# Row sums of adj in the first layer: the running adds on GpSimd instead of VectorE

## What is computed

```python
def _L0_gnn_ref(h, adj, W_neigh, b_neigh, W_self, b_self):
    deg = jnp.sum(adj, axis=1, keepdims=True) + 1e-05
    h_neigh = (adj / deg) @ h
    return relu(h_neigh @ W_neigh.T + b_neigh + h @ W_self.T + b_self)

def _L1_gnn_ref(x, adj, W, b):
    rowsum = adj.sum(axis=1)
    d_inv_sqrt = jnp.where(rowsum > 0, rowsum ** (-0.5), 0.0)
    support = (d_inv_sqrt[:, None] * adj * d_inv_sqrt[None, :]) @ x
    return relu(support @ W + b)

x = _layernorm(x + _L0_gnn_ref(x, adj, ...))
x = _layernorm(x + _L1_gnn_ref(x, adj, ...))
```

## Time and profile before

| | us |
|---|---|
| median of 3 runs | 800.73 |
| lowest, highest | 800.4, 802.11 |
| span of the profiled execution | 800.8 |

### The profile page before, as it was taken

One profiled execution on the slowest core, in us unless ns is written; L12 is line 12 of the kernel. 1 busy time (PEld: TensorE's weight loads), 2 busy tenths in 40 slices (PEclk: granted clock), 3 DMA queues, 4 the chain that ended last, 5 costly groups with the idle time before them and its releaser, 6 DMA issues.

```text
span 800.8 us, 11034 instructions
## 1 busy us (share of the span) xinstructions
PE 782.1 (98%) x3704; PEld 653.0 (82%) x3704; DVE 577.4 (72%) x868; ACT 386.9 (48%) x528; POOL 0.3 (0%) x6
## 2 busy tenths in 40 slices
PE   7899999999999999999999999999999999999995
PEld 4678888888888888888888888888888888888884
DVE  5799989899898998989966554555546455554643
ACT  3463745536446364454554545445444544545451
POOL 0000000000000000000000000000000000000000
PEclk9999999999999999999999999999999999999998
DMA  8767574755647556465565575746575574657540
GB/s 258 274 252 239 179 244 154 253 183 166 236 155 236 193 174 236 157 233 189 181 227 165 175 255 174 250 162 237 180 236 187 171 246 162 236 180 239 180 158 27
DMA packets 54459, 160.93 MB, mean 201 GB/s; under 512 B 5024, under 2 KB 18464, under 8 KB 54432
## 3 DMA queue, kind: packets, MB, share of 16 engines
q1 hardware_dynamic: 46224, 152.46, 56.6%
q10 hardware_dynamic: 8208, 8.13, 2.9%
HBM read 152.17 MB, written 8.39 MB: 201 GB/s over the span
## 4 chain that ended last, share of the span: by engine, by line
PE 94%; DMA 2%; DVE 2%; ACT 1%; issue 0%; SPq 0%
PE ps_main L675 84%; PE ps_epi L613 8%; DMA raw<-adj_t 2%; PE ps_main L657 1%; PE ps_epi L634 1%; DMA tt<-x_nat 1%; DVE lo L389 0%; DVE acc L565 0%; ACT hi L256 0%; PE ps_epi L693 0%; DVE tt L436 0%; DVE stats L585 0%; DVE tt L419 0%; DVE xs L389 0%; ACT tt L359 0%
## 5 line engine op out<-in xcount | busy, mean ns | idle before, releaser
L256 ACT ACTIVATE hi<-raw 128x1024 fp32r<-128x1024 f32 x254 | 269.4, 1061 | 352.8 <-PE ps_main L675 327.8
L389 DVE TENSOR_TENSOR lo<-raw,hi 128x1024 fp32r<-128x1024 f32 x254 | 310.4, 1222 | 145.3 <-ACT hi L256 145.2
L675 PE MATMUL ps_main<-hi,xs 128*128 128x512 f32 x1136 | 366.3, 392 | 4.3 <-DVE lo L389 4.3
L675 PE MATMUL ps_main<-hi,zs 128*128 128x512 f32 x896 | 283.0, 390 | 0.0
L675 PEld LDWEIGHTS ps_main<-hi,xs 128*128 128x128 f32 x1136 | 214.2, 189 | 49.3 <-DVE lo L389 3.6
L675 PE MATMUL ps_main<-lo,xs 128*128 128x512 f32 x568 | 222.4, 392 | 0.0
L675 PEld LDWEIGHTS ps_main<-hi,zs 128*128 128x128 f32 x896 | 168.3, 188 | 34.3
L675 PE MATMUL ps_main<-lo,zs 128*128 128x512 f32 x448 | 174.7, 390 | 0.0
L565 DVE TENSOR_TENSOR acc<-acc,raw 128x1024 f32<-128x1024 f32 x112 | 136.3, 1217 | 0.0
L675 PEld LDWEIGHTS ps_main<-lo,xs 128*128 128x128 f32 x568 | 107.3, 189 | 20.0 <-issue 0.2
L675 PEld LDWEIGHTS ps_main<-lo,zs 128*128 128x128 f32 x448 | 84.2, 188 | 16.3
(11 more groups left out here) (74 smaller groups left out, 322.7 us busy)
## 6 DMA issues: line engine op xcount, KB each, us to landing
raw<-adj_t SPq DMA_DIRECT2D x256, 512.0 KB, 3.3
res<-x_nat SPq DMA_DIRECT2D x11, 512.0 KB, 6.4
xt_sb<-xt SPq DMA_DIRECT2D x8, 512.0 KB, 5.0
x_scratch<-tt ACTq DMA_DIRECT2D x8, 512.0 KB, 6.2
res<-x_scratch SPq DMA_DIRECT2D x8, 512.0 KB, 6.0
out<-tt ACTq DMA_DIRECT2D x7, 512.0 KB, 6.4
tt<-x_nat SPq DMA_DIRECT2D x4, 512.0 KB, 6.4
acc<-x_nat SPq DMA_DIRECT2D x2, 256.0 KB, 3.6
```

The costliest lines, as they stand in the source:

```text
L256: return act.activation(dst, src, ACT.Copy)
L389: return dve.tensor_tensor(dst, src, hi_part.bitcast(f32), ALU.subtract)
L675: last = pe.matmul(ps[:, f, :], stationary(layer, part, jt, f), mov[:, slot(u), cols], start=(jt == 0 and i == 0), stop=(jt == JT - 1 and ...
```

## The change

The 15 adds of each block in the first layer leave VectorE's program and stand in GpSimd's, in a loop of their own with the same arithmetic and order. Each now waits for its transfer (`raw_full`) and for the add before it. At the start of a block after the first, GpSimd waits for `rs_copied`, so that the half of acc which it takes has been read; for this rs_copied begins one higher (a memset that counts it), and TensorE's wait for it moves up by one. The first block's x goes through acc's second half on its way in, so GpSimd also waits for `xl_ready` and `unit_done` there. SP's and ScalarE's programs are the same as before.

```diff
-        marks = sb("marks", [P, 3])
+        marks = sb("marks", [P, 4])
...
             pool.memset(marks[:, 0:1], 0.0).then_inc(tt_stored, 16)
+            pool.memset(marks[:, 3:4], 0.0).then_inc(rs_copied, 1)
+
+            def one_block(layer, b, parity, epi):
+                if layer == 1:
+                    return
+                g0 = b * NU
+                k0 = b * (NU // RING)
+                a = acc[:, parity, :]
+                if not is_first(b):
+                    pool.wait_ge(rs_copied, b)
+                    pool.wait_ge(xl_ready, 1)
+                    pool.wait_ge(unit_done, WHOLE)
+                for u in range(NU):
+                    pool.wait_ge(raw_full[slot(u)], (k0 + (u // RING + 1)) * 16)
+                    if u == 1:
+                        pool.tensor_tensor(a, raw[:, slot(0), :], raw[:, slot(1), :], ALU.add)\
+                            .then_inc(acc_done, 2)
+                    if u > 1:
+                        pool.wait_ge(acc_done, g0 + u)
+                        pool.tensor_tensor(a, a, raw[:, slot(u), :], ALU.add).then_inc(acc_done, 1)
+
+            one_block(0, 0, 0, None)
+            with pool.Fori(1, NB - 1, 2) as b:
+                one_block(0, b, 1, None)
+                one_block(0, b + 1, 0, None)
+            one_block(0, NB - 1, 1, None)
...
                     place(u, 1)
-                    if layer == 0:
-                        a = acc[:, parity, :]
-                        if u == 1:
-
-
-                            dve.tensor_tensor(a, raw[:, slot(0), :], raw[:, slot(1), :], ALU.add)\
-                               .then_inc(acc_done, 2)
-                        if u > 1:
-                            dve.wait_ge(acc_done, g0 + u)
-                            dve.tensor_tensor(a, a, raw[:, slot(u), :], ALU.add).then_inc(acc_done, 1)
                     place(u, 2)
...
-                        pe.wait_ge(rs_copied, e + 1)
+                        pe.wait_ge(rs_copied, e + 2)
```

## The result

| | before | after |
|---|---|---|
| median, us | 800.65 | 883.51 |
| lowest, highest, us | 800.4, 802.11 | 880.73, 884.01 |
| span of the profiled execution, us | 800.8 | 882.2 |

The changed kernel is slower: the ratio is 1.1022, 95% interval 1.1005 to 1.1039. Some 83 us were lost. The forecast was 886 us, in a range of 845 to 905 us for this case alone and of 799 to 905 us overall.

A forecast was written before the change was run, and what follows sets the result against it. TensorE was taken as the bound. Alternating SBUF access adds 11.4 us in each of 8 blocks: 800.8 + 91 - 6 of used-up lead = 886 us; range 845 to 905 for this case, 799 to 905 overall.

The forecast's parts named there:

- VectorE's adds are worth nothing in seven blocks, 1.2 us in the first: First layer: removing VectorE's 120 adds saves 0 beside a full TensorE in seven blocks, 1.2 us in the first block.
- Turns: First layer: GpSimd adds and VectorE's two-SBUF-operand instructions alternate, so their times add up; 11.4 us more a block, chance 0.58.
- GpSimd's add, 2.22 us: Each moved add on GpSimd: two passes of 1.06 us plus 0.10 us, between ends of 1.22 and 3.18 us.
- Handing over, 2.4 us a block: First-layer block: some 30 passes between GpSimd and VectorE at 0.08 us each, 2.4 us in all.
- the sum of a block: First-layer block: VectorE's two-operand work 26.1, GpSimd's adds 33.3 and passes between engines 2.4, 61.8 us against 50.4.
- The first block, 11 us: First block of the first layer: its work ends at 71 us instead of about 60, the same 11 us loss.
- The lead of 6 us used up at the end: End of the first layer: the splits' 6.5 us of advance over TensorE is consumed instead of kept, -6 us.
- The span as the metric: Whole kernel: nothing is shown outside the profiled span, which equals the median to 0.1 us, so it stands for the metric.
- The signs: Profile after: adds 3 us and more on meeting, TensorE busy 50 of 62 us, lo waits 80 to 90, second layer 46.5.
- rival (c): First layer: the engines share SBUF in part, overlap 8 to 11 us, blocks 52 to 54, time 807 to 823; chance 0.10.
- six small instructions: VectorE in each first-layer block: newton, d_cur, d_all, nmr, inv_root counted as two-operand SBUF work, 0.16 us each, 1.0 in all.
- Rival (b): First block: the 3.13 us TensorE wait and lower clock go too, 795 us; chance 0.10, including no loss with a little more.

## Why the prediction was right, point by point

- **VectorE's adds are worth nothing in seven blocks, 1.2 us in the first.** Right: with GpSimd only writing, every block behind the first is 50.39 us as before, and 1.7 us are gained in all (799.2 us).
- **Turns.** Right, and shown in three ways: by the instructions' own lengths, by the width, and by reading against writing. The Trainium skill's rule (page "SBUF — State Buffer", section "Who interferes with whom": the one that starts first keeps the shared ports for its whole length) agrees with these rows, 3.47 us for a lo behind an add of 2.40. The instructions with one operand in PSUM, which I had left out of the sum, were never longer: 25 of the 32 of L455 began while an add was running, and none took over 0.418 us.
- **GpSimd's add, 2.22 us.** It is 2.40. This term was too small by 0.18 us, 2.7 us a block. Two passes came near: GpSimd's own copy of one operand takes 1.04 us, and twice that is 2.08. Whether the add really makes two passes is not shown. The estimate of 2.25 us from the Trainium skill (page "GPSIMD Engine Reference", section "Elementwise — side-by-side cycle accounting") is low as well; the measured 2.40 decides.
- **Handing over, 2.4 us a block.** Nothing of it shows. L462, 0.42 us alone, ends 0.28 us behind the add that it waited for, and VectorE's own instructions follow one another 1.14 us apart rather than 1.22. That makes the sum of a block 24.7 + 36.0 = 60.7 us where I had 61.8. The add was 2.7 us a block too short; the hand-overs, 2.4, and the distance of VectorE's instructions, 1.4, were too long. That these nearly cancel is luck. Six of the seven blocks measured 60.0 to 61.6 us.
- **The first block, 11 us.** 11.9 us between the spans, about 13 by the medians.
- **The lead of 6 us used up at the end.** The last of the seven blocks takes 56.6 us, the six ahead of it 60.9 on average, so 4.3 us were given back. That they are the lead is not shown.
- **The span as the metric.** The profiled execution of the changed kernel has a span of 882.2 us and a time of 884.01: 1.8 us lie outside it, which I had put at nothing. That the span before equalled the median was chance: its execution was about 2 us slower than the median.
- **The signs.** The second layer stayed at 46.48 us a block and the adds reached 3.80 us, as described. TensorE's waits for lo are 54.7 us, not 80 to 90, and it is busy for 53 to 54 us of a block, not 50: its mean hi*x_hi and hi*x_lo matmul is 400 ns for 392, so part of the loss stands in longer matmul records. The lower clock, on which I did not count, came in one of the blocks shown (0.98) and left it at 61.6 us.
- **A slip in rival (c).** An overlap of 8 to 11 us makes a block 50.8 to 53.8 us, not 52 to 54. No forecast hangs on it.
- **What I had wrong in the picture.** I counted six small instructions as colliding because they read two tensors. L468 and L472, which read one tensor of two and four columns, wait too (2.38 us at most). And the sum of the two-operand work alone is not the price: with eight adds the runs came out 10 to 28 us above the ranges that I had worked out from it. VectorE's order, which puts its other work behind the waits, is my explanation. For this change the sum came within 0.4 us of the average block. That it did so here and not there is again partly luck.
- **Rival (b),** 3.13 us in the start: it did not come with this change, as forecast, but the reason that I gave against it was too strong: three reorderings of the start shortened the wait or removed it, though in the first two that transfer is still issued at 14.3 and 14.8 us, behind TensorE's first units.

## What to carry to other kernels

Before moving elementwise work to GpSimd to relieve VectorE, add up the two engines' SBUF-reading work in the stage: an add on GpSimd took 2.40 us here for 1.22 on VectorE, and it is paid on VectorE's queue as well, so a move that frees 18 us in a 50 us block cost 10. GpSimd's writes beside lo, and VectorE work with an operand in PSUM beside GpSimd's adds, ran for free. And where a profile says that an engine is 91% busy beside a full TensorE, freeing it is worth only what TensorE waits for it, here some 1.7 us; look for the waits instead, most of which a reordering of the start removed for 0.5 to 0.6%.

## What the runs showed of the hardware that I had not expected

- A VectorE TENSOR_SCALAR of 2 columns took up to 2.38 us for its wait for GpSimd (0.16 alone), but RECIPROCAL of 4 columns in SBUF (L434) ran beside an add four times and never took more than 0.167 us.
- GpSimd's writes are not free for everything. In the run with memsets, the maxima of these rows (by line, min/median/max ns) are far above their own time, while lo's is not:

```profile
L463 DVE SCALAR_TENSOR_TENSOR tt<-tt,res x64: 407/422/1805, 68.9 to 790.6; 128x256 f32<-128x256 f32 x64
L463 DVE DVE_READ_ACCUMULATOR tt<-tt,res x64: 76/82/1453, 69.3 to 790.9; 128x1 f32 x64
...
L469 DVE TENSOR_SCALAR nmean<-sums x30: 159/161/1920, 75.5 to 760.3; 128x2 f32<-128x2 f32 x30
```

  The z split is the same kind of instruction on tiles of the same size, without an accumulator, and kept its own time in that run (mean 476 ns for 479 before):

```profile
L505 DVE SCALAR_TENSOR_TENSOR zs<-tt,d_cur,zs 128x256 f32 (+1 forms) x28 | 12.2, 476 | 0.0
```

  That points at the accumulator's output as what makes L463 wait; it was not tried by itself.
- GpSimd's add: 1.27 us for 512 columns, 1.84 for 768, 2.40 for 1024, so about 2.2 ns a column and 0.15 us besides.
